# Moving the fourth group's router on VectorE, ScalarE and TensorE, and the first group's last expert chunk

## The chip, the cores and the metric

One Trainium2 chip, one of its cores. The metric is the device time of one execution in microseconds (us), the median of the runs shown.

## The reference

For each of 4 sequences of 1024 positions and 1024 channels, a decayed mix runs along the positions in both directions, and its result `y` goes into a linear layer with a bias and sixteen rank-16 experts, of which a router picks two for each position:

```
nf, df = forward scans of  a*decay + e^k*v  and  b*decay + e^k
nb, db = the same scans backward
num = nf + nb - e^k*v + e^(u+k)*v ;  den = df + db - e^k + e^(u+k)
y   = sigmoid(r) * num / max(den, 1e-8) * (0.8 + 0.2*tf)
h   = silu(y @ rw1.T + rb1) ; logits = h @ rw2.T + rb2 + gates
coeff = softmax over the top 2 logits, at their places, else 0
out = x + y @ W.T + bias + sum_e coeff_e * (y @ A_e.T) @ B_e.T
```

Here k = v = `f`, and r = `x`. All is fp32.

## The kernel before, in words

Channels lie on the partitions. A **unit** is one sequence's block of 128 channels over all 1024 positions: 4 sequences x 8 blocks = 32 units, and **step** s handles unit s. The five engines each run a program of their own, written out by hand in loops over s; order on an engine is the order of the code, and semaphores tie them together.

In step s VectorE (DVE) runs, on tiles of 128x1024: `ratio` of the unit before (L807), `forward` (the denominator's scan, L769), `forward_num` (L773), `backward_den` (L778), `p2` (L783), `sum_den` (L788), `scale_e` of the next unit (L756), `backward_num` (L800). ScalarE (ACT) makes exponentials (`exp_k` L411, `exp_uk` L417), the sigmoid of r (L452), one column's rescale ahead of each backward scan (`scale_end_den`, `scale_end_num`, L440), the reciprocal through Ln and Exp (`inverse`, L463 and L465), and the rounded half of y (`split_hi`, L428). GpSimd (POOL) makes a product (`p1`, L669), a sum (L644), y itself (L650) and the remainder `y_lo` (`split_lo`, L679). SyncE (SP) issues loads and stores in the order of its own loop; `load_r(s + 1)` stands there behind stores of the group that ends.

Each sequence has two **groups** G of 512 positions, 8 groups in all. TensorE (PE) works group by group, each product as three matmuls of 128x512 (`three`, L983 to L985: hi x hi, lo x hi, hi x lo). For a group it runs:

- `hid` (L1014, L1015): the router's hidden sums over 8 blocks, and `low_rank`: y @ A.T, 2 x 8 blocks. Groups with an even number run units 0 to 4 of their sequence first and the last three as those become ready (`unit_in` waits for y_lo).
- `base`: y @ W.T, an output tile j at a time, 8 blocks each (groups 0 and 1: 4, the other half was made earlier); `bank_in` waits until a PSUM bank was evacuated.
- `logits` (L1052), which waits for the silu of the hidden sums (`h_ready`); `turn` (L1059), the transposition of the routing coefficients, which waits for `cat_ready`; `spread` (L1067), which hands each coefficient to its 16 ranks.
- `expert` for each output tile, which needs the weighed low-rank rows, split in `wx_hi` and `wx_lo`.

For this DVE has four **router tasks** in each group: `hidden` (L826), `silu` (L835), `routing` (L846 to L880, 25 small instructions that end in `cat`), `weigh` (L887, xa times the spread coefficients). After which of its own operations each stands is set by the tables `hidden_at`, `silu_at`, `routing_at` and `weigh_at`; `evacs_at` does this for the evacuations (L821) of finished output tiles. ACT has `low_rows` (L483), `sigmoid_z` (L487), `copy_xa` (L498), `exp_gap` (L502), `copy_turned` (L511, `cat_t`) and `split_wx` (L516); POOL has `wx_lo` (L692). The fourth group (G = 3) has its routing and weighing in step 20; the fifth (G = 4) in step 25; the first (G = 0) in step 9; the second in step 12.

How many base blocks of tile 2 PE runs ahead of `turn` is the table `ahead`. The weights come in 13 chunks through staging tiles; chunk 12, the second half of the expert weights, is rounded on ACT (`weights_hi`, L479) and its remainder made on POOL (`weights_lo`, L634), at steps that the tables `hi_mid_steps` and `lo_late_steps` name.

## Time and profile before

| what | value |
|---|---|
| median of 3 runs | 674.62 us (674.05 to 674.89) |
| the profiled execution's own time | 672.5 us |
| its span | 670.7 us |
| PE busy | 593.9 us, 89% |
| DVE busy | 517.5 us, 77% |
| ACT, POOL busy | 54%, 55% |
| mean granted TensorE clock | 0.964 |

Times of the trace count from the start of the span. A row of a timeline has an instruction's start, its length, the engine and line, and in brackets how long the engine stood idle before it and what released it. Matmuls overlap: the next one starts before the row's length is over.

### The profile page before, as it was taken

What the parts mean: (1) busy time and instruction counts of PE and PEld (TensorE: products, weight loads), DVE (VectorE), ACT (ScalarE), POOL (GpSimd) and SP (SyncE); (2) the same over time, 40 slices, a digit from 0 to 9 for tenths busy, and PEclk for the clock granted to TensorE, in tenths of its full rate; (3) what the DMA queues carried; (4) which work ended last, traced back from release to release, by engine and by line L of the source; (5) the groups of instructions that cost most, each with busy time, mean ns of one, the idle gap of its engine ahead of it and who ended that gap; (6) DMA issues with size and microseconds to landing.
All of it is one profiled execution on the core that took longest, in us unless ns stands there. A gap on an engine that the chain in (4) does not pass through costs nothing.

```text
span 670.7 us, 6900 instructions
## 1 busy us (share of the span) xinstructions
PE 593.9 (89%) x2554; PEld 478.4 (71%) x2554; DVE 517.5 (77%) x579; ACT 360.1 (54%) x429; POOL 367.8 (55%) x182
## 2 busy tenths in 40 slices
PE   0153689979999989999999959999999999999997
PEld 0142567758878757888778848888788888888786
DVE  7999999999999999999699989999699322031202
ACT  6788899855854676566456584558455220020100
POOL 1799999868857864666266764585347301000100
PEclk9967789989999999999999979999999999999999
DMA  5324467525755811237231622345231502050112
GB/s 196 125 92 155 145 231 235 165 92 124 191 125 111 232 66 63 95 105 243 78 121 52 216 98 78 110 139 175 79 110 48 156 1 90 5 158 0 34 61 79
DMA packets 33249, 78.45 MB, mean 117 GB/s; under 512 B 4736, under 2 KB 4928, under 8 KB 33216
## 3 DMA queue, kind: packets, MB, share of 16 engines
q1 hardware_dynamic: 30912, 73.82, 33.6%
q0 software_dynamic: 2304, 4.20, 4.2%
q8 instruction: 20, 0.33, 0.2%
q14 instruction: 13, 0.11, 0.1%
HBM read 57.03 MB, written 20.97 MB: 116 GB/s over the span
## 4 chain that ended last, share of the span: by engine, by line
PE 64%; DVE 18%; POOL 6%; ACT 5%; issue 4%; DMA 2%; SPq 0%; DVEq 0%; ACTq 0%; POOLq 0%
PE acc L983 20%; PE acc L984 19%; PE acc L985 19%; DVE mix L769 3%; DVE mix L773 3%; DVE mix L778 3%; DVE mix L800 2%; PE acc L1014 2%; DVE eu L788 2%; PE acc L1015 2%; DVE yr L807 1%; DVE mix L756 1%; PE acc L1052 1%; POOL y_lo L679 1%; DVE xo L821 1%
## 5 line engine op out<-in xcount | busy, mean ns | idle before, releaser
L983 PE MATMUL acc<-y_hi,wa_hi 128*128 128x512 f32 x638 | 258.5, 405 | 54.1 <-POOL y_lo L679 49.3
L984 PE MATMUL acc<-y_lo,wa_hi 128*128 128x512 f32 x638 | 254.3, 399 | 0.0
L985 PE MATMUL acc<-y_hi,wa_lo 128*128 128x512 f32 x638 | 254.0, 398 | 0.0
L983 PEld LDWEIGHTS acc<-y_hi,wa_hi 128*128 128x128 f32 x638 | 123.7, 194 | 86.4 <-POOL y_lo L679 50.7
L985 PEld LDWEIGHTS acc<-y_hi,wa_lo 128*128 128x128 f32 x638 | 123.2, 193 | 26.7
L984 PEld LDWEIGHTS acc<-y_lo,wa_hi 128*128 128x128 f32 x638 | 123.9, 194 | 25.2
L669 POOL TENSOR_TENSOR mix<-mix,kv 128x1024 f32<-128x1024 f32 x30 | 71.9, 2396 | 77.8 <-DVE mix L756 77.8
L821 DVE SCALAR_TENSOR_TENSOR xo<-acc,bias_sb,xo 128x512 f32<-128x512 f32 x64 | 46.8, 735 | 73.9 <-PE acc L985 73.7
L679 POOL TENSOR_TENSOR y_lo<-yr,y_hi 128x1024 fp32r<-128x1024 f32 x31 | 76.4, 2464 | 37.5 <-ACT y_hi L428 37.5
L692 POOL TENSOR_TENSOR wx_lo<-xa,wx_hi 128x512 fp32r<-128x512 f32 x16 | 21.2, 1346 | 119.6 <-ACT wx_hi L516 119.6
L650 POOL TENSOR_TENSOR yr<-mix,yr 128x1024 f32<-128x1024 f32 x31 | 74.2, 2394 | 4.9 <-DVE yr L807 2.7
L644 POOL TENSOR_TENSOR mix<-mix,kv 128x1024 f32<-128x1024 f32 x31 | 74.4, 2399 | 3.5 <-DVE mix L800 3.5
L778 DVE TENSOR_TENSOR_SCAN mix<-d_ps,mix 128x1023 f32<-128x1023 f32 x32 | 74.5, 2329 | 0.5 <-ACT mix L440 0.5
L769 DVE TENSOR_TENSOR_SCAN mix<-d_ps,mix 128x1024 f32<-128x1024 f32 x32 | 72.9, 2278 | 1.4 <-POOL mix L669 1.3
L800 DVE TENSOR_TENSOR_SCAN mix<-d_ps,mix 128x1023 f32<-128x1023 f32 (+1 forms) x32 | 73.7, 2302 | 0.0
L773 DVE TENSOR_TENSOR_SCAN mix<-d_ps,mix 128x1024 f32<-128x1024 f32 x32 | 72.5, 2267 | 0.0
L463 ACT ACTIVATE eu<-eu,tiny 128x1024 f32<-128x1024 f32 (+1 forms) x32 | 34.4, 1076 | 48.6 <-DVE eu L788 48.4
L417 ACT ACTIVATE eu<-kv,u_sb 128x1024 f32<-128x1024 f32 x32 | 35.8, 1118 | 35.7 <-DVE yr L807 35.6
L983 PE MATMUL acc<-wx_hi,wb_hi 128*128 128x512 f32 x128 | 50.7, 396 | 3.0 <-POOL wx_lo L692 3.0
L985 PE MATMUL acc<-wx_hi,wb_lo 128*128 128x512 f32 x128 | 50.5, 395 | 0.0
L984 PE MATMUL acc<-wx_lo,wb_hi 128*128 128x512 f32 x128 | 50.4, 394 | 0.0
L526 ACT ACT_TABLE_LOAD x35 | 44.9, 1283 | 1.4 <-PEq L1253 0.7
(126 smaller groups left out, 702.1 us busy)
## 6 DMA issues: line engine op xcount, KB each, us to landing
kv<-f_cm SPq DMA_DIRECT2D x32, 512.0 KB, 3.6
yr<-x_cm SPq DMA_DIRECT2D x32, 512.0 KB, 3.9
out<-xo SPq DMA_DIRECT2D x64, 256.0 KB, 3.8
xo<-x_cm SPq DMA_DIRECT2D x64, 256.0 KB, 3.8
out<-xo POOLq DMA_DIRECT2D x16, 256.0 KB, 6.2
xa<-w_base SPq DMA_DIRECT2D x5, 512.0 KB, 3.5
xo<-w_base SPq DMA_DIRECT2D x3, 512.0 KB, 4.9
xo<-w_router_a SPq DMA_DIRECT2D x2, 480.0 KB, 3.6
```

The costliest lines, as they stand in the source:

```text
L644: nc.gpsimd.tensor_tensor(n_of(g)[:, t], num_of(g)[:, t], kv[:, g % 2, t], ALU.add).then_inc(n_ready, 1)
L650: nc.gpsimd.tensor_tensor(yr[:, g % 2, t], n_of(g)[:, t], yr[:, g % 2, t], ALU.mult).then_inc(y_ready, 1)
L669: nc.gpsimd.tensor_tensor(num_of(g), den_of(g), kv[:, g % 2, :], ALU.mult).then_inc(p1_ready, 1)
L679: nc.gpsimd.tensor_tensor(slots(y_lo, g), yr[:, g % 2, :].rearrange("p (h t) -> p h t", h=2), slots(y_hi, g).bitcast(fp32), ALU.subtract). ...
L769: nc.vector.tensor_tensor_scan(den_of(g), decay(g, T), den_of(g), 0.0, ALU.mult, ALU.add).then_inc(den_fwd, 1)
L773: nc.vector.tensor_tensor_scan(num_of(g), decay(g, T), num_of(g), 0.0, ALU.mult, ALU.add).then_inc(num_fwd, 1)
L778: nc.vector.tensor_tensor_scan(rev(den_of(g)), decay(g, T - 1), rev(den_of(g)), den_of(g)[:, T - 1:T], ALU.mult, ALU.add).then_inc(den_bwd, 1)
L800: nc.vector.tensor_tensor_scan(a[:, stop - 1::-1], decay(g, stop), a[:, stop - 1::-1], a[:, stop:stop + 1], ALU.mult, ALU.add).then_inc(nu ...
L821: nc.vector.scalar_tensor_tensor(out=xo[:, e % XBUF, :], in0=acc[:, bank, :], scalar=bias_sb[:, j:j + 1], in1=xo[:, e % XBUF, :], op0=ALU. ...
L983: nc.tensor.matmul(out_ap, wh, yh, start=start, stop=False)
L984: nc.tensor.matmul(out_ap, wh, yl, start=False, stop=False)
L985: return nc.tensor.matmul(out_ap, wl, yh, start=False, stop=stop)
```

## The change

Eight edits, all in order alone: no instruction is added, removed or changed in size.

- **Fourth group (G = 3), step 20.** DVE: `routing` goes from behind `forward_num` to behind `backward_den`, `weigh` from behind `backward_den` to behind `scale_e`. ACT: `exp_gap` and `copy_turned` go behind `scale_end_num` and `exp_k`, `split_wx` behind `inverse`. POOL: `wx_lo` goes behind `p1`. PE: the three base blocks ahead of `turn` go behind it (`ahead` 3 becomes 0).
- **Fifth group (G = 4), on PE.** The low-rank blocks of units 5 to 7 run beside each unit's `hid`, no longer after the third; four base blocks of tile 1 go from behind `logits` to ahead of it.
- **First group (G = 0).** Chunk 12 is rounded in step 8 rather than 9; POOL takes its remainder ahead of `y_lo`. ACT runs `split_wx` ahead of `exp_k`. PE runs one base block fewer ahead of `turn` (`ahead` 8 becomes 7).

```diff
@@ -120,9 +120,9 @@
         load_steps = [[], [2, 3], [4], [5], [7], [9], [11], [12]]
         load_late_steps = [[], [], [], [6], [8], [10]]
         hi_steps = [[1], [2], [3, 4], [5, 6], [7, 8], [9], [10], [11]]
-        hi_mid_steps = [[], [], [], [], [], [], [], [], [], [12]]
-        lo_steps = [[0], [1], [2], [3], [5], [7], [9], [10], [11]]
-        lo_late_steps = [[], [], [], [4], [6], [8], [], [], [], [12]]
+        hi_mid_steps = [[], [], [], [], [], [], [], [], [12]]
+        lo_steps = [[0], [1], [2], [3], [5], [7], [9], [10], [11], [12]]
+        lo_late_steps = [[], [], [], [4], [6], [8]]
 
         def chunks_at(table, s):
             return table[s] if s < len(table) else []
@@ -201,10 +201,10 @@
         silu_at = {(first_step(G) + 1, AFTER_RATIO): G for G in range(GROUPS) if G not in (SPLIT, 4)}
         silu_at |= {(THIRD, AFTER_FWD): SPLIT, (FIFTH, AFTER_BWD_NUM): 4}
         routing_at = {(first_step(G) + 1, AFTER_FWD): G for G in (0, 5, 6, 7)}
-        routing_at |= {(first_step(G) + 1, AFTER_FWD_NUM): G for G in (1, 3)}
+        routing_at |= {(first_step(1) + 1, AFTER_FWD_NUM): 1, (first_step(3) + 1, AFTER_BWD_DEN): 3}
         routing_at |= {(THIRD, AFTER_FWD_NUM): SPLIT, (FIFTH + 1, AFTER_RATIO): 4}
         weigh_at = {(first_step(G) + 1, AFTER_FWD_NUM): G for G in (0, 4, 5, 6, 7)}
-        weigh_at |= {(first_step(1) + 1, AFTER_P2): 1, (THIRD, AFTER_BWD_DEN): SPLIT, (first_step(3) + 1, AFTER_BWD_DEN): 3}
+        weigh_at |= {(first_step(1) + 1, AFTER_P2): 1, (THIRD, AFTER_BWD_DEN): SPLIT, (first_step(3) + 1, AFTER_SCALE): 3}
 
         def summed(G):
             return G + 1 - (G > SPLIT)
@@ -577,18 +577,24 @@
                     if s == 0:
                         act.wait_ge(recip_ready, 1)
                     scale_end_den(s)
-                if routed and G != 4:
+                if routed and G not in (3, 4):
                     exp_gap(G)
                 if 0 < s <= UNITS and not late_split:
                     split_hi(s - 1)
-                if routed:
+                if routed and G != 3:
                     copy_turned(G)
                 if s < UNITS and not routed and not late_sigmoid:
                     exps()
                 if s < UNITS:
                     scale_end_num(s)
+                if routed and G == 0:
+                    split_wx(G)
+                if routed and G == 3:
+                    exp_gap(G)
                 if s + 1 < UNITS:
                     exp_k(s + 1)
+                if routed and G == 3:
+                    copy_turned(G)
                 for n in chunks_at(hi_mid_steps, s):
                     weights_hi(n)
                 if s == 3:
@@ -596,7 +602,7 @@
                 if s in part_steps:
                     for p in range(part_steps[s][0], part_steps[s][1]):
                         drain_part(p)
-                if routed:
+                if routed and G not in (0, 3):
                     split_wx(G)
                 if s < UNITS and late_sigmoid:
                     sigmoid_r(s)
@@ -607,6 +613,8 @@
                     if s == 0:
                         act.wait_ge(gains_ready, 2)
                     inverse(s)
+                if routed and G == 3:
+                    split_wx(G)
                 for n in chunks_at(hi_steps, s):
                     weights_hi(n)
                 if s in part_steps:
@@ -726,10 +734,12 @@
                     add_out(e)
                 for n in chunks_at(lo_late_steps, s):
                     weights_lo(n)
-                if q == 1 and G != SPLIT:
+                if q == 1 and G not in (SPLIT, 3):
                     split_wx(G)
                 if s + 1 < UNITS and s + 1 not in OWN_P1:
                     p1(s + 1)
+                if q == 1 and G == 3:
+                    split_wx(G)
                 if s == CB - 2:
                     pool.wait_ge(late_in, 16 * 8)
                     nc.gpsimd.tensor_tensor(rbg[:], rb2_sb[:], gates_sb[:], ALU.add).then_inc(rbg_ready, 1)
@@ -1153,8 +1163,11 @@
                     for kc in range(first, CB):
                         unit_in(G, kc)
                         hid(G, kc)
+                        if G == 4:
+                            for a in range(2):
+                                low_rank(G, a, kc)
                     for a in range(2):
-                        for kc in range(first, CB):
+                        for kc in range(CB if G == 4 else first, CB):
                             low_rank(G, a, kc)
                     if G < SPLIT:
                         logits(G)
@@ -1162,13 +1175,17 @@
                         bank_in(G, 3)
                     for kc in range(first if G == 4 else k0, CB):
                         base(G, 0, kc)
+                if G == 4:
+                    bank_in(G, 4)
+                    for kc in range(4):
+                        base(G, 1, kc)
                 if G != 1:
                     logits(G)
                 if G != SPLIT:
                     bank_in(G, 4)
-                    for kc in range(k0, CB):
+                    for kc in range(4 if G == 4 else k0, CB):
                         base(G, 1, kc)
-                ahead = {0: CB, SPLIT: CB - 1, 3: 3}.get(G, k0)
+                ahead = {0: CB - 1, SPLIT: CB - 1}.get(G, k0)
                 if ahead > k0:
                     pe.wait_ge(xa_copied, 2 * G + 1)
                     for kc in range(k0, ahead):
```

In the rows below an engine's instructions stand in the order of its program. DVE, step 20, before; L880 ends `routing`, L778 is `backward_den`, L887 is `weigh`:

```order
276 L878 CAST cat<-d_ps 128x8x16
277 L880 TENSOR_TENSOR cat<-d_ps,cat 128x8x16
278 L778 SCALAR_TENSOR_TENSOR mix<-d_ps,mix 128x1023
279 L887 TENSOR_TENSOR xa<-acc,xa 128x512 x2
280 L783 SCALAR_TENSOR_TENSOR kv<-eu,kv 128x1024
281 L788 SCALAR_TENSOR_TENSOR eu<-eu,mix 128x1024
282 L756 TENSOR_SCALAR mix<-mix,delta_g 128x1024
283 L800 SCALAR_TENSOR_TENSOR mix<-d_ps,mix 128x1023
284 L807 SCALAR_TENSOR_TENSOR yr<-eu,limit_g,yr 128x1024
```

And now (each line number is 10 higher):

```order
276 L885 TENSOR_TENSOR d_ps<-first_hit,d_ps 128x64
277 L888 CAST cat<-d_ps 128x8x16
278 L890 TENSOR_TENSOR cat<-d_ps,cat 128x8x16
279 L793 SCALAR_TENSOR_TENSOR kv<-eu,kv 128x1024
280 L798 SCALAR_TENSOR_TENSOR eu<-eu,mix 128x1024
281 L766 TENSOR_SCALAR mix<-mix,delta_g 128x1024
282 L897 TENSOR_TENSOR xa<-acc,xa 128x512 x2
```

`backward_den` no longer stands between `cat` and `weigh` but ahead of all of `routing`; between `cat` and `weigh` stand `p2`, `sum_den` and `scale_e` instead.

ACT, step 20, before; L502 is `exp_gap`, L511 `copy_turned`, L516 `split_wx`:

```order
257 L498 COPY xa<-acc 128x512 x2
258 L440 ACTIVATE mix<-mix,rdelta_g 128x1
259 L502 ACTIVATE ex<-gap 128x4
260 L428 ACTIVATE y_hi<-yr 128x2x512
261 L511 ACTIVATE cat_t<-acc 64x512
262 L440 ACTIVATE mix<-mix,rdelta_g 128x1
263 L411 ACTIVATE mix<-kv 128x1024
264 L516 ACTIVATE wx_hi<-xa 128x512 x2
265 L463 ACTIVATE eu<-eu,tiny 128x1024
266 L465 ACTIVATE eu<-eu,log_gain_g 128x1024
```

And now:

```order
257 L498 COPY xa<-acc 128x512 x2
258 L440 ACTIVATE mix<-mix,rdelta_g 128x1
259 L428 ACTIVATE y_hi<-yr 128x2x512
260 L440 ACTIVATE mix<-mix,rdelta_g 128x1
261 L502 ACTIVATE ex<-gap 128x4
262 L411 ACTIVATE mix<-kv 128x1024
263 L511 ACTIVATE cat_t<-acc 64x512
264 L463 ACTIVATE eu<-eu,tiny 128x1024
265 L465 ACTIVATE eu<-eu,log_gain_g 128x1024
266 L516 ACTIVATE wx_hi<-xa 128x512 x2
```

The rounding of y (L428) no longer stands behind `exp_gap`, `exp_k` (L411) stands ahead of `copy_turned`, and the reciprocal (L463, L465) ahead of `split_wx`.

POOL, step 9, before and now; `wb_lo` is chunk 12's remainder:

```order
55 L669 TENSOR_TENSOR mix<-mix,kv 128x1024
56 L644 TENSOR_TENSOR mix<-mix,kv 128x1024
57 L650 TENSOR_TENSOR yr<-mix,yr 128x1024
58 L679 TENSOR_TENSOR y_lo<-yr,y_hi 128x1024
59 L634 TENSOR_TENSOR wb_lo<-xo,wb_hi 128x1024
60 L692 TENSOR_TENSOR wx_lo<-xa,wx_hi 128x512 x2
```

```order
55 L677 TENSOR_TENSOR mix<-mix,kv 128x1024
56 L652 TENSOR_TENSOR mix<-mix,kv 128x1024
57 L658 TENSOR_TENSOR yr<-mix,yr 128x1024
58 L642 TENSOR_TENSOR wb_lo<-xo,wb_hi 128x1024
59 L687 TENSOR_TENSOR y_lo<-yr,y_hi 128x1024
60 L700 TENSOR_TENSOR wx_lo<-xa,wx_hi 128x512 x2
```

`wb_lo` (L634, now L642) stands ahead of `y_lo` (L679, now L687) rather than right ahead of `wx_lo`.

## Rows read from the trace of the kernel before

**Rows 1.** Busy time, share of the span and instructions by engine, part 1 of the page

```profile
PE 593.9 (89%) x2554; PEld 478.4 (71%) x2554; DVE 517.5 (77%) x579; ACT 360.1 (54%) x429; POOL 367.8 (55%) x182
```

**Rows 2.** Waits, longest first: engine, line, releaser; us, times, longest us

```profile
PE acc L1014 <- POOL y_lo L679: 6.8, 1, 6.8
```

**Rows 3.** Timeline: start us, us, engine, line, operation, output<-input, idle before and releaser

```profile
384.51 0.43 SPq L323 DMA_DIRECT2D yr<-x_cm  x1
393.32 0.79 PE L1014 MATMUL acc<-y_hi,wr 128*128 128x512 f32 x1 [6.75 <-POOL y_lo L679]
```

**Rows 4.** Busy time of each engine by stretch; then granted TensorE clock (PEclk), DMA share, GB/s

```profile
130.00:134.00 4.00, 2.46 (x15) 1.89 (x14) 4.00 (x4) 3.96 (x5) 3.42 (x3) 1.00 0.55 184
139.00:142.00 3.00, 1.48 (x10) 0.96 (x9) 3.00 (x4) 1.92 (x4) 0.66 (x1) 0.98 0.44 141
142.00:145.00 3.00, 3.00 (x9) 2.35 (x8) 3.00 (x2) 1.90 (x3) 2.06 (x1) 0.50 0.09 34
393.00:398.00 5.00, 4.68 (x11) 3.71 (x12) 4.33 (x5) 3.73 (x5) 1.59 (x2) 0.51 0.35 108
```

**Rows 5.** Timeline, the fourth group's first and later expert blocks and first stores' evacuations

```profile
337.28 0.44 PE L983 MATMUL acc<-wx_hi,wb_hi 128*128 128x512 f32 x1
343.27 0.72 DVE L821 SCALAR_TENSOR_TENSOR xo<-acc,bias_sb,xo 128x512 f32<-128x512 f32 x1
366.23 0.39 PE L983 MATMUL acc<-wx_hi,wb_hi 128*128 128x512 f32 x1
371.16 0.72 DVE L821 SCALAR_TENSOR_TENSOR xo<-acc,bias_sb,xo 128x512 f32<-128x512 f32 x1
```

**Rows 6.** Timeline of step 20, on ACT, DVE and PE

```profile
322.48 0.30 ACT L440 ACTIVATE mix<-mix,rdelta_g 128x1 f32<-128x1 f32 x1
322.65 0.23 DVE L846 TENSOR_TENSOR lg<-acc,rbg 128x64 f32<-128x64 f32 x1 [1.90 <-PE acc L1052]
326.52 2.34 DVE L778 TENSOR_TENSOR_SCAN mix<-d_ps,mix 128x1023 f32<-128x1023 f32 x1
330.16 0.40 PE L1059 MATMUL acc<-ident_r,cat 128*64 128x128 f32 x4
332.63 0.50 PE L1067 MATMUL acc<-cat_t,expand_r 32*128 32x512 f32 x2
333.17 1.29 DVE L887 TENSOR_TENSOR xa<-acc,xa 128x512 f32<-128x512 f32 x2 [4.32 <-PE acc L1067]
337.64 2.33 DVE L800 TENSOR_TENSOR_SCAN mix<-d_ps,mix 128x1023 f32<-128x1023 f32 x1
341.07 2.27 DVE L769 TENSOR_TENSOR_SCAN mix<-d_ps,mix 128x1024 f32<-128x1024 f32 x1
```

**Rows 7.** Timeline of steps 24 and 25, on DVE and ACT

```profile
395.19 0.74 DVE L826 SCALAR_TENSOR_TENSOR fan<-acc,rb_sb,fan 64x512 f32<-64x512 f32 x1 [0.67 <-ACT fan L483]
399.33 0.68 DVE L835 TENSOR_TENSOR fan<-acc,fan 64x512 f32<-64x512 f32 x1 [0.48 <-ACT acc L487]
403.34 0.23 DVE L846 TENSOR_TENSOR lg<-acc,rbg 128x64 f32<-128x64 f32 x1 [2.13 <-PE acc L1052]
407.20 2.28 DVE L769 TENSOR_TENSOR_SCAN mix<-d_ps,mix 128x1024 f32<-128x1024 f32 x1
410.67 0.58 ACT L511 ACTIVATE cat_t<-acc 64x512 fp32r<-64x512 f32 x1
```

**Rows 8.** Timeline, last expert chunk and weighed low-rank rows of the first group

```profile
126.81 0.59 ACT L483 COPY fan<-acc 64x512 f32<-64x512 f32 x1 [1.53 <-PE acc L1015]
142.94 2.38 POOL L634 TENSOR_TENSOR wb_lo<-xo,wb_hi 128x1024 fp32r<-128x1024 f32 x1 [3.28 <-ACT wb_hi L479]
148.27 0.50 PE L983 MATMUL acc<-wx_hi,wb_hi 128*128 128x512 f32 x1 [2.32 <-POOL wx_lo L692]
```

**Rows 9.** Timeline, second group's router on PE and DVE

```profile
192.91 0.40 PE L1059 MATMUL acc<-ident_r,cat 128*64 128x128 f32 x4
195.92 1.29 DVE L887 TENSOR_TENSOR xa<-acc,xa 128x512 f32<-128x512 f32 x2 [1.16 <-PE acc L1067]
```

## Prediction

> **What bounds the kernel now.** I read the page's part 1 first: PE is busy for 593.9 of 670.7 us, 89% [rows 1]. So the kernel costs PE's work, plus what PE idles, plus what its clock loses. I then listed PE's waits. Those before step 8 are the start, and this change does not touch them. After that one stands out: 6.8 us on `y_lo` before L1014 [rows 2]. The timeline places it: PE has nothing to do for 6.75 us before 393.32, until the last unit of the third sequence (unit 23) has its `y_lo` [rows 3]. The windows show what follows: from 393 to 398 the granted clock is 0.51, the 1.2 GHz level [rows 4]. At full clock matmuls start 0.23 us apart: from 337.28 to 366.23 there are 126 of them [rows 5]. Five us at half clock hold what 2.6 would, so about 2.4 us more are lost. After 393.32 PE never waits again. Hence all of that pause and clock loss, 9.2 us, could be won, and no more in that place.
>
> Which chain is late there? DVE's. Unit 23 comes out of a chain of steps that DVE runs without a break, but for two waits of step 20: 1.90 us for `logits` and 4.32 us for `spread` [rows 6]. What shortens step 20 moves every later unit.
>
> **The change part by part, all in the old trace's clock.**
>
> *Step 20 on DVE.* Now `backward_den` comes first. It needs its rescaled column, which ACT makes at 322.48 [rows 6], so it starts at 322.7, no earlier than `routing` did. Of the 1.90 us wait nothing is won. Then `backward_den` takes 2.25 us, `routing` 3.87 us (322.65 to 326.52), and `cat` is ready at 328.8, 2.3 later than before. PE has three base blocks less ahead of `turn`: it used to reach it at 330.16, now 9 x 0.227 = 2.04 earlier, at 328.1. It waits 0.7 us. From `turn` to the first weighing took 333.17 - 330.16 = 3.0 us, of which ACT's `cat_t` and three base blocks are the filling; both stay, so `weigh` may start at 331.8. DVE is busy meanwhile: `p2`, `sum_den` and `scale_e` took from about 334.4 to 337.64, 3.2 us, a little less without `wx_lo` beside them, so it arrives at 331.8 as well. The 4.32 us are gone. `forward` of unit 21 started at 341.07 and now starts at 341.07 - 4.4 = 336.7, **4.4 us earlier**. `exp_k`, which ACT now runs ahead of `copy_turned`, falls in time in which ACT waited for PE. On POOL `p1` is ahead of `wx_lo`, which ends about 336.9; PE reaches the experts at 337.28 + 0.7 = 338.0, so this is covered.
>
> *What is late next.* DVE's first evacuation (343.27 before) would come at 338.9, but PE starts its expert block only at 338.0, and the block needs 1.6 to 1.7 us: it waits 0.8, leaving 3.6. The second place is the fourth evacuation at 371.16 [rows 5]. DVE would be there at 367.6. Its expert block starts on PE at 366.23 + 0.7 and is done at 368.5. Another 0.95 us goes, leaving **2.65 us** for unit 23. SP is not in the way: the load of r (384.51) stands behind a store that waits for DVE's last evacuation, and moves with it [rows 3].
>
> *Fifth group on PE.* Unit 23 is ready at 393.32 - 2.65 = 390.7. Meanwhile PE has 12 more matmuls, the low-rank blocks of units 21 and 22, 2.7 us: its pause shrinks from 6.75 to about 0.7 us (arrival 386.57 + 0.7 + 2.7 = 390.0), and with it, I think, the clock loss. But PE then runs into DVE again. Between `hid` of the last unit and `logits` there are still 27 matmuls, 6.1 us, enough to cover the silu chain (hid, ACT, DVE, ACT, DVE: about 5.6 us: it ended at 400.0, and `hid` near 394.4 [rows 7]). Behind `logits` only four base blocks are left ahead of `turn` where there were eight. On DVE two waits shrink: 0.67 for `hidden` and 2.13 for `logits` [rows 7], against about 0.6 for `logits` and 0.3 for `exp_gap` now. So step 25's `forward` comes 2.65 + 2.8 - 1.0 = **4.4 us** earlier than 407.20. PE in turn waits some 1.7 us for `cat` and 1.5 us for `cat_t`: `cat_t` stood at 410.67 [rows 7], and on ACT it is behind the rescale that waits for `forward`. From `spread` on PE is 4.4 us early as well, and nothing later made it wait. This can be seen from the other side too: had DVE gained nothing, `spread` would stand where it stood, and the 12 early matmuls would only have moved the pause.
>
> *First group.* Chunk 12 is rounded in step 8, in the 1.53 us in which ACT stood idle before 126.81. POOL's remainder (142.94, 2.38 us) goes into its wait for `y_hi`, and `wx_lo` no longer waits behind it [rows 8]. It is ready near 144.8, before PE, which arrives at 145.95. The 2.32 us pause goes, and with it seven matmuls at half clock, 1.4 us: PE is 3.7 us early. But it meets DVE in the second group. `silu` and `routing` there wait for nothing but DVE's own turn, so PE first waits about 0.6 for `silu` and then, due at `turn` at 192.91 - 3.1 = 189.8, another 1.5 for `cat`. What is left is that DVE no longer waits 1.16 us for `spread` [rows 9]. DVE then paces everything up to step 20, so **1.2 us** of the 3.7 arrives. Bounds: 0.2 (a clock fall at that wait, which puts `spread` back where it was) and 3.7. I take 1.2 because DVE is continuous up to 194.76, 1.16 before `weigh`. The base block moved behind `turn` in the first group is worth nothing: `weigh` there starts behind `forward_num`, not behind `spread`.
>
> *The clock.* From 139 to 142 PE was busy for 1.48 of 3.00 us, with pauses below 0.8 us each, and from 142 to 145 the clock was 0.50 [rows 4]. This is the first group's `turn` and `spread`. Seven slowed matmuls cost 7 x 0.2 = 1.4 us. The fifth group's `turn` and `spread` now have pauses of 1.7 and 1.5 us around them, longer ones than the first group's, and nearly the same little work. I count one such fall, **1.4 us lost**; the bounds are none and two. The Trainium skill, TensorE: Matmul & The Clock Gate, in "Why this matters for your kernels", warns of long idle gaps between bursts alone; by that the new waits are harmless and the sum would be 1.4 us better, which is rival 1. The trace does not agree: the pauses from 139 to 142 were below 0.8 us each, and the clock fell behind them [rows 4].
>
> **Sum.** 4.4 + 1.2 - 1.4 = 4.2 us. The profiled execution took 672.5 us, 1.8 us more than its span, and would take 668.3. It lies 2.1 us below the median of the runs, 674.62; against that the forecast is 674.62 - 4.2 = **670.4 us**.
>
> **Rivals.**
>
> 1. *No clock fall.* PE's new waits do not lower the clock. Gain 4.4 + 1.2 = 5.6: 669.0 us. For it: from 130 to 134 PE was busy for 2.46 of 4 us, a wait of 1.5 us among them, and the clock stayed at 1.00 [rows 4]. Against: the stretch from 139 to 145. The Trainium skill, TensorE: Matmul & The Clock Gate, in "Why this matters for your kernels", would have this case. Chance 0.28.
> 2. *Only half of DVE's gain comes through.* The wait at `turn` in step 20 or 12 brings a fall of its own, and evacuations wait for PE a little longer. 1.4 us of each lost: gain 1.5 to 2.5, 672.6 us. Chance 0.13.
> 3. *The edits do not act* (no change). Should `cat_t` or `exp_gap` in step 20 be held up on ACT, `weigh` would come at 336 rather than 331.8 and DVE would gain nothing; the fifth group then gains nothing either, as shown. Within 1.3 us of 674.62. Chance 0.08.
> 4. *Slower: PE becomes late in the fourth group.* DVE's fourth evacuation has room: it stood at 371.16, and the expert block that it needs was done at 367.8. So up to 3.3 us of delay on PE cost DVE nothing beyond the gain. If the clock falls at the wait at `turn` (0.7 + 1.4), and PE then finds `wx_lo` not ready because `p1` is ahead of it on POOL (0.5 to 1), and the clock falls again (1.4), the delay is 4.0 to 4.5 us. That is past the point of 3.3 by about 1, and with the fifth group's own fall of 1.4 the result is 2 us slower: 676.6. For it: `turn` comes right behind `logits` and four to eight base blocks now. Against: PE has 27 matmuls between `spread` and the experts. Chance 0.06.
>
> The main case, with one fall, has 0.45.
>
> **How the numbers follow.** A measurement of this kernel can tell 0.2%, about 1.3 us, from no change. Cases 1, 2 and the main one are faster by more: 0.28 + 0.13 + 0.45 = 0.86; I take 0.85. No change 0.08, slower 0.07. The range goes from 667.8 (rival 1 with a better share of the first group's 3.7) to 673.4 (the lower half of rival 2); outside are rivals 3 and 4 and the far gain, some 0.2.
>
> **What would show it.** In the new trace: DVE has no wait before `weigh` in step 20 above 0.5 us, and `forward` of unit 21 comes 5 to 6 us before 341.07 (1.2 from the first group included). PE's pause before the last `hid` of the fifth group is about 1 us, and the clock behind it stays at 1.00. New PE waits appear at `turn` of groups 2, 4 and 5 and before `spread` of group 5. The wait for `wx_lo` in the first group is gone. I am wrong if the wait before `weigh` of step 20 stays, if PE waits over 3 us at unit 23, or if the fifth group's `turn` and `spread` cost more than 5 us.

## The result, and the profile after

The changed kernel took 666.67 us (median of 5 runs, 666.16 to 668.64), the kernel before 674.05 us (5 runs, 672.86 to 674.89). The ratio is 0.9897, with a 95% interval of 0.988 to 0.9914: 5.8 to 8.1 us faster. The forecast was 4.2 us faster, with 667.8 us as the lower end of the range. The direction and most places were right; the size was not. The time lies outside the range.

The profiled execution of the change was the slowest of its five, 668.64 us, with a span of 666.8 us. That matters below. Its page, part 1, against [rows 1] (PEld are TensorE's weight loads, which overlap PE):

```profile
PE 589.0 (88%) x2554; PEld 474.3 (71%) x2554; DVE 516.8 (77%) x579; ACT 359.3 (54%) x429; POOL 367.1 (55%) x182
```

VectorE and TensorE in step 20, by the timeline of the change (start, length, engine and line, operation, idle before and releaser). These rows answer to [rows 6]; line numbers of VectorE are 10 higher now:

```profile
317.04 2.27 DVE L779 TENSOR_TENSOR_SCAN mix<-d_ps,mix 128x1024 f32<-128x1024 f32 x1
323.87 2.35 DVE L788 TENSOR_TENSOR_SCAN mix<-d_ps,mix 128x1023 f32<-128x1023 f32 x1 [2.38 <-ACT mix L440]
...
330.11 0.45 PE L1069 MATMUL acc<-ident_r,cat 128*64 128x128 f32 x4 [0.94 <-DVE cat L890]
333.15 1.29 DVE L897 TENSOR_TENSOR xa<-acc,xa 128x512 f32<-128x512 f32 x2 [0.16 <-PE acc L1077]
...
337.78 2.28 DVE L779 TENSOR_TENSOR_SCAN mix<-d_ps,mix 128x1024 f32<-128x1024 f32 x1
```

The step went as predicted. `backward_den` comes first and waits for its rescaled column, 2.38 us (1.90 was VectorE's wait before). PE waits 0.94 us at `turn`, where 0.7 was forecast. The 4.32 us wait before `weigh` is 0.16. From unit 20's forward scan to unit 21's it took 24.76 us before and takes 20.74 now. Unit 21's scan itself, at 337.78, is 3.3 us ahead of 341.07, and 4.8 in a second profile of the change (336.29); the forecast was 5 to 6, the first group's 1.2 included.

The two evacuations that were to wait for TensorE do so, and unit 23 reaches PE almost in time. The same timeline, against [rows 5] and [rows 3]:

```profile
340.85 0.75 DVE L831 SCALAR_TENSOR_TENSOR xo<-acc,bias_sb,xo 128x512 f32<-128x512 f32 x1 [0.79 <-PE acc L995]
369.42 0.75 DVE L831 SCALAR_TENSOR_TENSOR xo<-acc,bias_sb,xo 128x512 f32<-128x512 f32 x1 [0.56 <-PE acc L995]
...
386.50 1.06 ACT L452 ACTIVATE yr<-yr 128x1024 f32<-128x1024 f32 x1 [0.41 <-DMA yr<-x_cm]
391.22 0.50 PE L1024 MATMUL acc<-y_hi,wr 128*128 128x512 f32 x1 [0.31 <-POOL y_lo L687]
```

The waits are 0.79 and 0.56 us (0.8 and 0.95 forecast), and PE's pause before the fifth group's last `hid` is 0.31 us (0.7 forecast, 6.75 before).

In the fifth group, against [rows 7]:

```profile
396.75 0.68 DVE L845 TENSOR_TENSOR fan<-acc,fan 64x512 f32<-64x512 f32 x1 [0.48 <-ACT acc L487]
399.12 0.22 DVE L856 TENSOR_TENSOR lg<-acc,rbg 128x64 f32<-128x64 f32 x1 [0.51 <-PE acc L1062]
403.49 0.45 PE L1069 MATMUL acc<-ident_r,cat 128*64 128x128 f32 x4 [1.45 <-DVE cat L890]
407.44 0.50 PE L1077 MATMUL acc<-cat_t,expand_r 32*128 32x512 f32 x2 [1.36 <-ACT cat_t L511]
```

VectorE's 2.13 us wait for `logits` is 0.51, and PE has the two new waits: 1.45 us at `turn` and 1.36 before `spread` (1.7 and 1.5 forecast). What did not come is the clock fall behind them. Busy time by stretch (PE, PEld, DVE, ACT, POOL, each with its count), then the granted clock, the DMA share and GB/s:

```profile
391.00:396.00 5.00, 4.78 (x21) 3.97 (x22) 4.84 (x5) 4.18 (x5) 2.08 (x2) 1.00 0.32 108
402.00:407.00 5.00, 2.63 (x14) 1.85 (x13) 4.86 (x8) 1.34 (x3) 0.02 (x1) 1.00 0.00 0
407.00:411.00 4.00, 3.56 (x16) 2.79 (x17) 3.85 (x4) 2.67 (x5) 3.69 (x3) 1.00 0.14 30
```

The clock is 1.00 throughout, where I had counted 1.4 us for a fall.

The first group is another matter, against [rows 4, 8]:

```profile
131.00:139.00 8.00, 6.48 (x20) 5.41 (x21) 7.61 (x30) 6.26 (x10) 7.92 (x4) 0.63 0.37 132
142.00:145.00 3.00, 2.23 (x10) 1.32 (x10) 1.85 (x3) 1.88 (x4) 0.41 (x1) 1.00 0.69 261
```

```profile
143.15 1.29 DVE L897 TENSOR_TENSOR xa<-acc,xa 128x512 f32<-128x512 f32 x2 [2.40 <-PE acc L1077]
147.19 0.50 PE L993 MATMUL acc<-wx_hi,wb_hi 128*128 128x512 f32 x1 [0.27 <-POOL wx_lo L700]
```

In this execution the clock fell in the stretch from 131 to 139, ahead of `turn`, and not at 142. PE came to `spread` late, VectorE waited 2.40 us for it, and step 10 began 2.4 us later than in the first profile of the kernel before, although the pause before the experts was down from 2.32 to 0.27 us. That profile had no fall from 131 to 139. So one execution of each is not enough to price a few us that hang on the clock.

### The profile page after: what moved, and what is told of

The parts are those of the page before. It is cut to its first block, busy times and chain, and to the rows that moved or that the text cites. A ratio compares the mean times of both kernels' runs of the same rounds, so it can differ in the third digit from the quotient of the medians.

```text
span 666.8 us, 6899 instructions
## 1 busy us (share of the span) xinstructions
PE 589.0 (88%) x2554; PEld 474.3 (71%) x2554; DVE 516.8 (77%) x579; ACT 359.3 (54%) x429; POOL 367.1 (55%) x182
## 4 chain that ended last, share of the span: by engine, by line
PE 49%; DVE 24%; DMA 7%; POOL 7%; ACT 6%; issue 6%; SPq 1%; POOLq 0%; ACTq 0%; DVEq 0%
PE acc L993 16%; PE acc L994 15%; PE acc L995 15%; DVE mix L788 5%; DMA out<-xo 4%; DVE mix L779 3%; DVE mix L783 3%; DVE mix L810 2%; DVE eu L798 2%; DVE yr L817 2%; POOL mix L652 1%; POOL mix L677 1%; DMA yr<-x_cm 1%; POOL y_lo L687 1%; DVE kv L793 1%
## 5 line engine op out<-in xcount | busy, mean ns | idle before, releaser
L993 PE MATMUL acc<-y_hi,wa_hi 128*128 128x512 f32 x638 | 256.9, 403 | 58.8 <-POOL y_lo L687 50.8
L687 POOL TENSOR_TENSOR y_lo<-yr,y_hi 128x1024 fp32r<-128x1024 f32 x31 | 76.3, 2460 | 33.3 <-ACT y_hi L428 33.3
L463 ACT ACTIVATE eu<-eu,tiny 128x1024 f32<-128x1024 f32 (+1 forms) x32 | 34.4, 1076 | 51.6 <-DVE eu L798 51.4
```

The lines of the kernel that those rows point to most:

```text
L687: nc.gpsimd.tensor_tensor(slots(y_lo, g), yr[:, g % 2, :].rearrange("p (h t) -> p h t", h=2), slots(y_hi, g).bitcast(fp32), ALU.subtract). ...
L993: nc.tensor.matmul(out_ap, wh, yh, start=start, stop=False)
```

## The experiments

Four theories were tested. *Chain*: VectorE's chain of units paces everything until the fifth group's `spread`, and TensorE after it. *PE*: only TensorE's own work and pauses count. *Clock*: what the sum missed is clock loss, and it differs between executions. *First group*: the missing gain lies there.

To compare executions I cut each trace into stretches: A from the start to unit 20's forward scan (L769), B to unit 21's, C to the end of unit 23's `y_lo`, D to the start of the fifth group's `spread`. The rest is the same for all but one of these kernels: 256.9 to 257.0 us up to the end of the last store's issue (256.4 in `e9_ahead_two`, which also changes what follows `spread`).

| kernel, one execution | A | B | C | D | B to D |
|---|---|---|---|---|---|
| before | 316.31 | 24.76 | 52.19 | 18.03 | 94.98 |
| before_again | 317.83 | 24.92 | 52.60 | 17.95 | 95.47 |
| e2_fifth | 316.57 | 24.93 | 51.69 | 18.51 | 95.13 |
| e4_first | 315.46 | 24.92 | 52.79 | 18.82 | 96.53 |
| e10_chunk_only | 317.13 | 24.44 | 52.81 | 18.59 | 95.84 |
| e5_filled | 316.38 | 24.94 | 52.77 | 17.54 | 95.25 |
| e1_fourth | 316.57 | 20.40 | 53.06 | 17.24 | 90.70 |
| e3_fourth_fifth | 315.88 | 20.24 | 53.05 | 16.49 | 89.78 |
| after | 317.04 | 20.74 | 53.39 | 16.27 | 90.40 |
| after_again | 315.98 | 20.31 | 53.13 | 16.42 | 89.86 |
| e8_weigh_up | 315.99 | 22.98 | 55.01 | 16.40 | 94.39 |
| e7_base_back | 316.44 | 19.77 | 53.08 | 18.70 | 91.55 |
| e6_turned_early | 315.80 | 20.05 | 53.08 | 15.02 | 88.15 |
| e9_ahead_two | 315.47 | 20.64 | 53.10 | 14.98 | 88.72 |

**The parts of the change, each alone.** `e1_fourth` has the fourth group's edits and nothing else:

```diff
-        routing_at |= {(first_step(G) + 1, AFTER_FWD_NUM): G for G in (1, 3)}
+        routing_at |= {(first_step(1) + 1, AFTER_FWD_NUM): 1, (first_step(3) + 1, AFTER_BWD_DEN): 3}
...
-                ahead = {0: CB, SPLIT: CB - 1, 3: 3}.get(G, k0)
+                ahead = {0: CB, SPLIT: CB - 1}.get(G, k0)
```

> Fourth group's edits alone (DVE, ACT, POOL and PE orders of step 20), nothing of the first and fifth group. Chain theory (VectorE's chain of units decides when unit 23 is ready): forward of unit 21 about 4.4 us earlier, unit 23 about 2.7 us earlier, PE's pause before the fifth group's last hid 6.75 - 0.7 - 2.7 = about 3.4 us with the clock fall behind it still there; 2.7 us faster than before. PE theory (only work and pauses of TensorE count, and the new wait at turn costs it): no more than 1 us faster.

Measured: 668.16 us, ratio 0.9921 (0.9895 to 0.9946), 5.3 us faster (3.6 to 7.1). Both theories had less: 2.7 us (chain) and at most 1 (PE). B is 4.4 shorter, as forecast. C and D are 0.5 longer and 1.1 shorter than the mean of the four with the old code there (`before`, `before_again`, `e4_first`, `e10_chunk_only`), so unit 23 is 3.9 us earlier and not 2.7, and less clock is lost behind a pause that is shorter than the expected 3.4 us:

```profile
390.09 0.80 PE L1022 MATMUL acc<-y_hi,wr 128*128 128x512 f32 x1 [2.72 <-POOL y_lo L685]
390.00:395.00 5.00, 4.91 (x16) 3.95 (x17) 4.66 (x5) 3.73 (x5) 1.59 (x2) 0.70 0.35 108
```

So most of the change's gain comes with the fourth group's edits alone.

`e2_fifth` has the two TensorE edits of the fifth group:

```diff
                         hid(G, kc)
+                        if G == 4:
+                            for a in range(2):
+                                low_rank(G, a, kc)
...
+                if G == 4:
+                    bank_in(G, 4)
+                    for kc in range(4):
+                        base(G, 1, kc)
                 if G != 1:
                     logits(G)
```

> Fifth group's two TensorE edits alone. Chain theory: unit 23 is ready when it was, 12 matmuls (2.7 us) go into the pause, but spread stands where it stood because cat_t does: 0 us, within 1. PE theory: 2.7 us of work are hidden in the pause for good, and are won: 2.7 us faster or more.

Measured: 673.19 us, ratio 0.9996 (0.9979 to 1.0013): no change, and 2.7 us faster is excluded. The pause shrinks from 6.75 to 3.52, and the time comes back as waits at `turn` and `spread`:

```profile
393.24 0.80 PE L1014 MATMUL acc<-y_hi,wr 128*128 128x512 f32 x1 [3.52 <-POOL y_lo L679]
407.75 0.45 PE L1059 MATMUL acc<-ident_r,cat 128*64 128x128 f32 x4 [1.09 <-DVE cat L880]
411.70 0.50 PE L1067 MATMUL acc<-cat_t,expand_r 32*128 32x512 f32 x2 [1.38 <-ACT cat_t L511]
```

That is the chain theory's case, and against the PE theory: 2.7 us of TensorE work moved into a pause wins nothing if VectorE and ScalarE deliver `cat_t` when they did.

`e3_fourth_fifth` has both:

> Fourth and fifth group's edits together, first group as before. Chain theory: 4.4 us faster, more than the two alone make together (2.7 and 0), because the fifth group's waits shrink only if both are there. If a part of what was not predicted (the change won about 7 us where 4.2 were forecast) lies here, it is 5.5 us or more; if it lies in the first group, 4.4.

Measured: 667.17 us, ratio 0.9905 (0.9883 to 0.9928), 6.4 us (4.9 to 7.9). That excludes 4.4 for the pair. The 6.4 is above the 5.5 that was set as the mark, so the missing part seems to lie mostly here and not in the first group, though the interval reaches below 5.5. The intervals of this kernel and of the one without the fifth group's edits overlap; in the traces B to D is 0.9 shorter with them.

`e4_first` has the first group's edits, `e10_chunk_only` only those of the tables for chunk 12:

```diff
-        hi_mid_steps = [[], [], [], [], [], [], [], [], [], [12]]
-        lo_steps = [[0], [1], [2], [3], [5], [7], [9], [10], [11]]
-        lo_late_steps = [[], [], [], [4], [6], [8], [], [], [], [12]]
+        hi_mid_steps = [[], [], [], [], [], [], [], [], [12]]
+        lo_steps = [[0], [1], [2], [3], [5], [7], [9], [10], [11], [12]]
+        lo_late_steps = [[], [], [], [4], [6], [8]]
```

> First group's edits alone (chunk 12 a step earlier, POOL and ACT order, one base block behind turn). Chain theory: the pause of 2.3 us before the experts goes, but only 1.2 us reaches the end. Rival: most of TensorE's 3.7 us reaches the end in a typical execution, 2.5 us or more. Third reading, from the profiled execution of the change, in which this group was 1.1 us later and not earlier: nothing, within 0.7 us, because the clock falls at another place.

> The kernel before, with chunk 12 alone a step earlier on ScalarE and ahead of y_lo on GpSimd (no other edit of the first group). The pause before the first group's experts shrinks from 2.3 to under 1 us. If this is what the first group's edits win, the ratio is the same as theirs, 0.997; if ScalarE's split_wx ahead of exp_k and the base block behind turn matter, it is between 0.998 and 1.

Measured: 672.13 us, ratio 0.9968 (0.9953 to 0.9983) for all of them, 1.1 to 3.2 us; 672.52 us, ratio 0.9981 (0.9968 to 0.9995) for the chunk alone. So the edits win something, against the third reading, and at least a part of it comes with the chunk (0.3 to 2.2 us); the intervals do not tell the two apart. Nor do they tell the forecast's 1.2 us from the rival's 2.5: the first interval holds both. In the traces A shows little: it is 316.0 on average in the seven executions that have all of the first group's edits, 316.6 in the six that have none, with 2.4 us between the shortest and the longest. The pause before the first group's experts is under 0.3 us with either set of edits, and 1.04 to 3.91 us in the six executions with none.

What TensorE gains in the first group is lost ahead of `logits` of the second, and not at `turn` as the prediction had it. The second profile of the change:

```profile
184.12 1.25 PE L1062 MATMUL acc<-rw_sb,fan 64*128 64x16 f32 x8 [1.77 <-DVE fan L845]
184.00:188.00 4.00, 3.88 (x14) 3.29 (x15) 4.00 (x3) 3.47 (x5) 3.92 (x4) 0.61 0.41 131
```

In all seven executions with all of the first group's edits TensorE waits 1.73 to 1.78 us for `silu` there (0.6 forecast), the clock falls behind it, and no wait is left at `turn` (1.5 forecast). VectorE does not wait for this group's `spread` in any of the seven. Its 1.16 us wait there [rows 9], on which the 1.2 us rest, came in four of the seven executions that have none or only the chunk's of these edits; in the other three (`before_again`, `e1_fourth`, `e10_chunk_only`) it waited nothing there and 1.57 to 1.61 us for the first group's `spread` instead.

**The same kernels again.** Both kernels were profiled a second time, unchanged.

> The kernel before, profiled a second time, unchanged. Step theory: the stretch from unit 20's forward scan to the fifth group's spread (94.98 us in the first profile, and longer than that in other kernels with the same code there) is not a fixed length; the clock loss behind PE's pause varies. It is then 95 to 97 us here, and the pause of 6.8 to 7.3 us costs 2.4 to 3.3 more by the clock. Rival: the profile was typical, 95.0 within 0.3.

> The changed kernel, profiled a second time, unchanged. If its first profile (span 666.8 us) was a late one because of the first group alone (unit 20's forward scan at 317.04), that scan comes at 315 to 316.3 here, and from it to the fifth group's spread it is 90.4 again, within 0.4, since nothing of the change's waits there lets the clock fall. Rival: the latter stretch moves by 1.4 us, a clock fall at the fifth group's turn.

These executions took 674.56 and 667.03 us. B to D of the kernel before was 95.47, and 95.84 and 96.53 in the two kernels that have the same code there; the first profile, on which the prediction was built, is the shortest of the four, 0.7 us below their mean of 95.7. For the change it was 89.86 after 90.40 (within 0.4 was expected), with PE's two new waits and no clock fall, and unit 20's scan came at 315.98, as expected. The kernel before, second profile, against [rows 3, 4]:

```profile
390.73 1.06 ACT L452 ACTIVATE yr<-yr 128x1024 f32<-128x1024 f32 x1 [1.25 <-DMA yr<-x_cm]
395.40 0.80 PE L1014 MATMUL acc<-y_hi,wr 128*128 128x512 f32 x1 [7.17 <-POOL y_lo L679]
395.00:402.00 7.00, 6.60 (x20) 5.26 (x21) 5.85 (x6) 5.72 (x7) 3.59 (x3) 0.66 0.26 77
```

The pause is 7.17 us, and ScalarE waited 1.25 us for the load of r where it waited 0.84 in the first. The load is issued behind VectorE's last evacuation; in the change ScalarE waited 0.41 us for it in one execution and not at all in the other.

**The clock behind the pause.** `e5_filled` is the kernel before with 24 more matmuls ahead of the fifth group's last `hid`:

```diff
+                        if G == 4 and kc == CB - 1:
+                            bank_in(G, 4)
+                            for _ in range(24):
+                                nc.tensor.matmul(acc[:, out_bank(G, 1), :], wa_hi[:, 0, ER:ER + P], y_of(G, 0)[0],
+                                                 start=True, stop=True)
                         unit_in(G, kc)
                         hid(G, kc)
```

> The kernel before, with 24 more matmuls of 128x512 (5.4 us) ahead of the fifth group's last hid, into a PSUM bank that is written anew later: they add work and fill the pause. Clock theory: the pause costs 2.4 to 3.3 us of clock beyond its own length; filled, that comes back, but only until the routing chain of VectorE is the later one (some 2 us): 2 us faster than before although it does more work. Rival (the pause costs only its length): 0 us, or slower.

Measured: 672.29 us, ratio 0.9985 (0.9971 to 0.9999), 1.0 us faster (0.1 to 2.0) although it computes 24 products more; 2 were expected. The filling was not complete:

```profile
394.14 0.50 PE L1014 MATMUL acc<-y_hi,wr 128*128 128x512 f32 x1 [1.88 <-POOL y_lo L679]
386.00:393.00 7.00, 6.26 (x28) 4.87 (x26) 6.20 (x4) 5.56 (x7) 3.99 (x3) 1.00 0.46 154
394.00:399.00 5.00, 4.86 (x14) 3.85 (x15) 4.78 (x5) 4.20 (x5) 2.07 (x2) 0.66 0.34 105
```

A pause of 1.88 us was left, and from 394 to 399 the clock was 0.66, not 0.51 as in [rows 4]. The direction fits the clock theory, but the interval ends at 0.1 us, next to the rival's nothing. The traces say it more sharply. At full clock 128x512 matmuls start 0.227 us apart, and behind the pause 0.427. The time above 0.227, added up over these matmuls, is the loss, and D can be set against it in the six executions whose TensorE order between unit 23's `y_lo` and `spread` is the old one:

| execution | pause | loss behind it | D | D less loss |
|---|---|---|---|---|
| e1_fourth | 2.72 | 1.4 | 17.24 | 15.8 |
| e5_filled | 1.88 | 1.7 | 17.54 | 15.8 |
| before_again | 7.17 | 2.1 | 17.95 | 15.8 |
| before | 6.75 | 2.2 | 18.03 | 15.8 |
| e10_chunk_only | 7.37 | 2.8 | 18.59 | 15.8 |
| e4_first | 7.35 | 3.0 | 18.82 | 15.8 |

What the clock loses there reaches the fifth group's `spread` in full. It is 2.1 to 3.0 us behind pauses of 6.75 to 7.37 us. In the three executions with the change's orders D is 16.3 to 16.5 with nothing lost.

**Where the gain of step 20 lies.** `e8_weigh_up` is the change, with one table entry back:

```diff
-(first_step(3) + 1, AFTER_SCALE): 3}
+(first_step(3) + 1, AFTER_BWD_DEN): 3}
```

> The changed kernel, with the fourth group's weigh alone put back on VectorE right behind routing, ahead of p2, sum_den and scale_e, so that it waits for spread again. Chain theory: VectorE waits about 3.2 us there, the stretch from unit 20's forward scan to unit 21's goes from 20.3 to about 23.3, and the change's gain shrinks by the same or a little less: 2.5 to 3 us slower than the change, 4 faster than before. Rival (the gain of the fourth group lies in ScalarE's, GpSimd's and TensorE's orders): within 1 us of the change.

Measured: 671.06 us, ratio 0.9961 (0.9948 to 0.9975), 4.3 us more than the change by the ratios (0.9961 - 0.9897 = 0.0064 of 674), where 2.5 to 3 were expected. Two things came at once:

```profile
331.40 1.29 DVE L897 TENSOR_TENSOR xa<-acc,xa 128x512 f32<-128x512 f32 x2 [3.08 <-PE acc L1077]
340.59 0.50 PE L993 MATMUL acc<-wx_hi,wb_hi 128*128 128x512 f32 x1 [2.87 <-POOL wx_lo L700]
342.45 0.75 DVE L831 SCALAR_TENSOR_TENSOR xo<-acc,bias_sb,xo 128x512 f32<-128x512 f32 x1 [1.21 <-PE acc L995]
...
372.46 0.75 DVE L831 SCALAR_TENSOR_TENSOR xo<-acc,bias_sb,xo 128x512 f32<-128x512 f32 x1 [2.02 <-PE acc L995]
341.00:346.00 5.00, 5.00 (x17) 3.95 (x16) 3.79 (x5) 2.44 (x4) 4.26 (x2) 0.66 0.38 116
```

VectorE waits 3.08 us for `spread` (3.2 expected), which lengthens B by 2.7. Since `scale_e` now is late, `p1` is late on GpSimd, and `wx_lo`, which the change put behind `p1`, keeps PE waiting for 2.87 us, with a clock of 0.66 from 341 to 346; the two evacuations then wait 1.21 and 2.02 us, and C is 1.9 longer. This is the wait that rival 4 spoke of. It came only where `weigh` stands early: with `weigh` back behind `backward_den`, GpSimd's new order costs time. No run has the orders of ScalarE, GpSimd or TensorE in step 20 alone, so their own shares are not known.

**The four base blocks.** `e7_base_back` is the change with the fifth group's four base blocks back behind `logits`:

```diff
-                if G == 4:
-                    bank_in(G, 4)
-                    for kc in range(4):
-                        base(G, 1, kc)
...
-                    for kc in range(4 if G == 4 else k0, CB):
+                    for kc in range(k0, CB):
                         base(G, 1, kc)
```

> The changed kernel, with the fifth group's four base blocks of tile 1 back behind logits; the low-rank blocks stay beside hid. Chain theory: VectorE's and ScalarE's order decides the fifth group's spread; PE now waits for silu ahead of logits (some 2 us) and no longer at turn, and the four blocks cover what they covered before: spread within 0.5 us of the change, so the same time within 1 us. Rival: logits comes 2 us later, all of routing with it, and the time is 1 to 2 us longer.

Measured: 668.26 us, ratio 0.9917 (0.9899 to 0.9936); the interval overlaps the change's. In the trace D is 2.3 us longer than in the change, while B, ahead of the edit, is the shortest of all (19.77, against 20.3 to 20.7), which makes up for a part of it in the time. PE waits 2.26 us for silu, and behind that the clock falls (matmuls 0.427 us apart, 2.7 us lost), with no wait at `turn` left:

```profile
395.79 1.58 PE L1062 MATMUL acc<-rw_sb,fan 64*128 64x16 f32 x8 [2.26 <-DVE fan L845]
396.00:400.00 4.00, 4.00 (x14) 3.41 (x14) 3.03 (x20) 3.50 (x5) 3.30 (x2) 0.52 0.42 133
400.00:403.00 3.00, 3.00 (x8) 2.31 (x7) 2.86 (x9) 0.00 (x0) 0.00 (x0) 0.50 0.00 0
```

So it was the rival that came nearer, with the clock as its means: one wait of 2.26 us with `logits` behind it was followed by 0.50, while two waits of 1.45 and 1.36 us with work between them were not, in any of five executions (both profiles of the change, `e2_fifth`, `e3_fourth_fifth`, `e8_weigh_up`). The second group's wait of 1.73 to 1.78 us ahead of its `logits` was followed by a fall as well, in seven executions of seven.

**A copy ahead of the rescale.** In `e6_turned_early` ScalarE runs the fifth group's `copy_turned` ahead of the rescale that waits for VectorE's forward scan:

```diff
                 if routed and G == 4:
                     exp_gap(G)
+                    copy_turned(G)
...
-                if routed and G != 3:
+                if routed and G not in (3, 4):
                     copy_turned(G)
```

> The changed kernel, with the fifth group's copy_turned on ScalarE right behind exp_gap, no longer behind the rescale that waits for VectorE's forward scan. PE's 1.36 us wait before the fifth group's spread should go. If that wait is on the path to the end: 1.3 us faster than the change, about 8 us faster than before (ratio 0.988). Rival: weigh stands behind forward_num on VectorE, comes no earlier, and PE waits for it or for wx_lo instead: same as the change.

Measured: 665.34 us, ratio to before 0.9874 (0.9851 to 0.9896). The median is 1.3 us below the change's, as expected, and so is D (15.02 against 16.3 to 16.5), though the intervals of the ratios overlap.

```profile
401.44 0.46 PE L1070 MATMUL acc<-ident_r,cat 128*64 128x128 f32 x4 [1.61 <-DVE cat L891]
401.93 0.59 ACT L511 ACTIVATE cat_t<-acc 64x512 fp32r<-64x512 f32 x1 [2.75 <-PE acc L1070]
403.62 0.29 ACT L440 ACTIVATE mix<-mix,rdelta_g 128x1 f32<-128x1 f32 x1 [1.09 <-DVE mix L780]
403.95 0.50 PE L1078 MATMUL acc<-cat_t,expand_r 32*128 32x512 f32 x2
```

`cat_t` comes at 401.93, ahead of the rescale at 403.62, and `spread` follows without a wait. `e9_ahead_two` adds two base blocks ahead of `turn` (`4: 2` in `ahead`) and `split_wx` ahead of `exp_k` for that group.

> The kernel with copy_turned early (665.3 us, ratio 0.9874), and in the fifth group two base blocks of tile 2 ahead of turn, where PE waits 1.6 us, and split_wx ahead of exp_k on ScalarE. PE's wait at turn goes to 0.3 us, 1.4 us; of it wx_lo lets about 1.0 through. Chain theory: 1 us faster than that kernel, ratio to before 0.986. Rival: nothing, since VectorE's weigh paces the experts.

Measured: 664.65 us, ratio 0.9876 (0.9858 to 0.9894): the same as without these, where 1 us was expected. The wait at `turn` is down to 0.25 us, but from unit 20's forward scan to the end it takes 345.1 us in both (88.72 + 256.39 and 88.15 + 256.99). This single execution had a B longer by 0.6, which may hide a small gain; 0.48 us of wait for `wx_lo` is new. Whether VectorE's `weigh` paces the experts, as the rival says, is not shown.

## Why the prediction was wrong

**Right, by its own steps.** What bounds the kernel: VectorE's chain up to unit 23, then TensorE with its pause and clock loss; `e1_fourth`, `e2_fifth`, `e8_weigh_up` and the table of D show it. Step 20: 4.4 us forecast; B is 24.8 on average in the six executions without the edit and 19.8 to 20.7 in the seven with it. The fifth group's edits alone: nothing. The new waits of the fifth group: 1.45 and 1.36 us (1.7 and 1.5 forecast). Rivals 2 to 4 did not come. (Rival 4's sum leaves out the first group's 1.2 us; with it 1 us slower would follow, not 2.)

**Wrong: two terms, both of the same sign, and the profile that they were taken from.** B to D was to become 3.0 us shorter (4.4 - 1.4). It became 95.7 - 90.0 = 5.7 shorter, where 95.7 is the mean of the four executions with the old code there and 90.0 that of the three with the change's (`after`, `after_again`, `e3_fourth_fifth`).

1. *"I count one such fall, 1.4 us lost."* It did not come in any of five executions with these waits. This is the largest single error. The fall was carried over from the first group's `turn` and `spread`, as they were in one profile. Rival 1, which had this right, got the smaller chance; its 5.6 us are still below the measured 5.8 to 8.1. Without the fall the forecast for D holds: unit 23 was to come 2.65 us earlier and `spread` 4.4, which leaves D 18.03 - 1.75 = 16.3; measured are 16.3 to 16.5.
2. *"Another 0.95 us goes, leaving 2.65 us for unit 23."* The waits of 0.8 and 0.95 us should have made C longer by 1.75. It grew from 52.6 to 53.2 on average, 1.2 less. The evacuations are nearly right: waits of 0.79 and 0.56 us put VectorE 1.57 us later. The other 1.0 us is the load of r, of which the prediction says only that it *"moves with"* its store. Its issue did move, by 1.57 us against unit 21's forward scan, but from issue to landing it then took less time:

```profile
yr<-x_cm SPq DMA_DIRECT2D x1, 512.0 KB, 4.1
yr<-x_cm SPq DMA_DIRECT2D x1, 512.0 KB, 3.7
```

These are lines of the DMA view at 384.5 in the kernel before and at 382.8 in the change; the last number is the time from issue to landing. It is 4.1 to 4.7 us in the four executions with the old code and 3.3 to 3.7 in the three with the change's, and ScalarE's wait for it fell from 0.84 to 1.46 us to between 0 and 0.41. The load is unit 24's r. Unit 23 does not need it, but on ScalarE the sigmoid of unit 24 stands ahead of unit 23's `y_hi`, and `y_lo` waits for that: in the first profile of the kernel before GpSimd had unit 23's y at 388.5, and `y_hi` began at 389.80. This second chain into unit 23, next to VectorE's, the prediction did not price. Why it took less time is not shown; in `e2_fifth`, with the old orders ahead of it, it took 3.6 us. Nor was `y_hi` ahead of the sigmoid tried.

3. *"The profiled execution took 672.5 us ... and would take 668.3."* The terms were differences to one execution, in which B to D was 0.7 us below the mean of its like: 0.4 in C, the wait for the load (0.84 against 1.25 on average), and 0.3 in D, the clock loss (2.2 against 2.5). This 0.7 is contained in the other terms. I shifted the level by 2.1 us to the median, but took the size of the terms as it stood.

The 2.7 us between 3.0 and 5.7 are thus 1.4 for the clock, 1.2 for C and 0.1 for the rest. That the measured 6.9 us also lie 2.7 above the forecast is in part chance: for the first group 1.2 us were forecast, and its own size is known only roughly. With its 0.6 (stretch A) to 2.2 (timed alone) the change should win 6.3 to 7.9; it won 5.8 to 8.1. Alone it measured 2.2 us, on top of the others 0.5 (0.9905 to 0.9897), and neither interval excludes 1.2. Its mechanism was in part another one: the wait for `silu` with a clock fall behind it, and no wait at `turn`.

## What to carry to other kernels

When two engines take turns waiting for each other, follow the chain that decides when the next unit is ready: moving small tasks behind work that does not need them shortened it by 4.4 us, while moving 2.7 us of another engine's work into a pause was worth nothing. Where a step hangs on the TensorE clock, look at more than one execution before pricing it, since the same instructions gave 95.0 to 96.5 us here. Look for every chain that ends in the step, loads included: one that ScalarE waited 0.84 us for, and that no edit touched, was worth 1.0 us here. An engine that runs in order can hold up a short, urgent copy behind a wait that the copy does not need; ask this of every task on the path, as ScalarE's `copy_turned` showed, and as the sigmoid ahead of unit 23's `y_hi` suggests.

## What the runs showed of the hardware

The clock falls at different places in different executions of the same program: behind the fifth group's pause the matmuls' spacing (0.427 us instead of 0.227) shows a loss of 2.2 us in one profile of the kernel before, 2.1 in the next and 3.0 in `e4_first`, which has the same code there. In the first group it stood at 1.00 from 131 to 139 in the first profile of the kernel before and fell at 142 [rows 4]; in the second it was 0.79 from 131 to 139:

```profile
131.00:139.00 8.00, 6.64 (x26) 5.53 (x27) 7.60 (x30) 6.12 (x9) 5.97 (x3) 0.79 0.32 101
```

PE at 2.63 us busy of 5.00, in a wait of 1.45 us and one of 1.36, kept its clock at 1.00 (the window from 402 to 407 above), and so it did in all five executions with such waits.

A single wait ahead of `logits` was less harmless, and not always alike. The first group has one of 1.50 to 1.55 us in all fourteen executions: from 134 to 138 the clock was then 1.00 in five of them and 0.50 to 0.68 in nine. The second group's of 1.73 to 1.78 us was followed by a fall in seven of seven, and the fifth group's of 2.26 in `e7_base_back` in the one execution that has it. What sets these apart from the waits at `turn` and `spread`, no run shows.
